# Decoder layer with windowed attention, WKV and a bit-linear MLP: the second tile's 8-bit rounding on VectorE, all calls placed anew

## The chip, the cores and the metric

The kernel runs on one core of a Trainium2 chip. The metric is the device time of one execution in microseconds; it is given as the median of several runs. TensorE (PE) multiplies, VectorE (DVE), ScalarE (ACT) and GpSimd (POOL) do the elementwise work, and SyncE (SP) only issues transfers.

## The reference

Sixteen batches of 256 tokens, 512 wide, in fp32, go through three residual steps: attention in overlapping windows of 128 tokens with sigmoid weights (16 heads of 32, one key and value head, quantised to 8 bits per batch), a WKV scan against a second input, and an MLP with ternary weights and rows quantised to 8 bits.

```python
x = x + attn(layernorm(x), wq, wk, wv, wo, ...)
x = x + wkv(w, u, layernorm(x), ctx)          # scan over 256 tokens
x = x + ffn(layernorm(x), w_gate, w_up, w_down, ln_weight)

def activation_quant(x):                       # per row, qn, qp = -128, 127
    s = qp / clip(max(abs(x), axis=-1), 1e-5)
    return clip(round(x * s), qn, qp) / s

def ffn(x):
    h = silu(bit_linear(x, w_gate)) * bit_linear(x, w_up)   # 256 x 2048
    h = ln_weight * h * rsqrt(mean(h * h) + 1e-6)
    return bit_linear(h, w_down)               # bit_linear quantises x and w
```

## The kernel before

Every engine has one program, a plain list of calls: a prologue, then `for i in range(4, B)` with 12 turns, then an epilogue. A turn works on five batches at once: b = i (queries, scores), w = i−1 (window blends, attention's output, WKV keys and scan), f = i−2 (WKV's quotient, first half of the MLP), g = i−3 (second half of the MLP), h = i−4 (output, store). The lists are written out by hand; each engine works in the order of its list, and semaphores (`Event`; `.at(f, t)` is the count that tile t of batch f brings) tie the lists together. So a call that waits holds up all that stands behind it in its list.

A batch has two tiles of 128 tokens (t = 0, 1), and the MLP's 2048 columns are four slices of 512 (n = 0 to 3). For each tile and slice: `gate_up` (TensorE, L653) makes the gate half and the up half in two banks; `silu` (ScalarE, L1022) and `hidden` (VectorE, L1526) make silu(gate)·up in `junk`; `squares` (ScalarE, L1027) sums its squares; `weigh_hidden` (GpSimd, L1858) multiplies by the norm's weight into `hid_w`. Per tile: `peak` (VectorE, L1535) takes the largest value of a row, `hidden_rstd` (GpSimd, L1875 to L1883) and `hidden_scale` (VectorE, L1542 to L1548) make the row's scale. Then `scale_hidden` (ScalarE, L996) multiplies the 128x2048 tile by it and adds MAGIC = 1.5·2^23, which rounds in fp32; `round_hidden` (ScalarE, L1006) subtracts MAGIC and writes bf16 into `hid_q`; `turn_hidden` (SP, L346) transposes a half of the tile by DMA, and `down` (TensorE, L673) multiplies. `round_hidden` of a batch must wait until the transposes of the batch before have read `hid_q`, `weigh_hidden` until the round has read `hid_w`. In the profile `hid_w`, `hid_q` and the transposed tiles all show as `work`.

Other names of the chain: `blend_windows` (L1426 to L1429) joins the attention windows, `wkv_back` (L632) transposes WKV's result, `attention_out` L613, `queries` L563, `scores` L582 (with `probs`, L957, on ScalarE); `wkv_keys` L623, `key_steps` (GpSimd, L1848), `exps` L1013, `values` L1448, `scan` L1459, `join` L1467; `rope` L1412 and `rotate` L1418 with transfers between them (`turn_queries`, L330); `keys_grid` L1398 to L1404, which needs the loads `next_keys` (L317, L318); `next_queries` (L305) loads xT once the buffer is read by `rotate(b,1)`; `weigh_windows` (GpSimd, L1841), `outputs` (GpSimd, L1889); `log_tables` (L961) loads ScalarE's table of logs. `spin(f,k,n)` (L665) makes n multiplies whose result nobody reads.

Of the kernel before, what the change touches and what calls it, by code (L numbers as in the profile page):

```python
# [14 lines left out]
NT = S // P  # L15
# [26 lines left out]
def build(nc, a, out, k_scratch, v_scratch):  # L42
# [150 lines left out]
    def event(name, per=1, unit=1):  # L193
# [62 lines left out]
    sq_sum, ms_set, h_norm, h_peak, h_scale, h_scaled, h_quant = [  # L256
        event(n, k * NT) for n, k in (("sq_sum", 1), ("ms_set", 3), ("h_norm", 1), ("h_peak", 1), ("h_scale", 4),
                                      ("h_scaled", 1), ("h_quant", 1))]
# [7 lines left out]
    def sync_program(sy):  # L266
# [72 lines left out]
        def turn_hidden(f, t, k):  # L339
            sy.wait_ge(h_quant.sem, h_quant.at(f, t))  # L340
# [41 lines left out]
        load_x(0)  # L382
        load_small()
        load_x(1)
        load_columns(0)
        load_columns(2)
        load_columns(1)
        load_x(2)
        load_x(3)
# [4 lines left out]
        store_trig(1)  # L394
        load_columns(5)
        load_x(7)
# [3 lines left out]
        load_keys(0)  # L400
        load_wq()
        load_columns(7)
        load_weights(GATE, 1)
        load_weights(GATE, 0)
        load_queries(0)
        store_trig(5)
        load_weights(GATE, 2)
        next_residual(1)
        store_trig(2)
        load_weights(GATE, 3)  # L410
        turn_queries(0, 0)
        turn_queries(0, 1)
        load_weights(UP, 0)
        load_weights(UP, 1)
        next_keys(0)
        load_weights(UP, 2)
        load_weights(UP, 3)
        next_queries(0)
        next_residual(0)
        store_trig(3)  # L420
        load_weights(DOWN, 1)
        load_weights(DOWN, 0)
        turn_queries(1, 0)
        store_trig(4)
        load_weights(DOWN, 2)
        turn_queries(1, 1)
        store_trig(6)
        load_weights(DOWN, 3)
        store_trig(7)
        next_queries(1)  # L430
        next_keys(1)
# [3 lines left out]
        turn_queries(2, 1)  # L435
        next_queries(2)
        next_keys(2)
        next_values(1)
# [3 lines left out]
        turn_queries(3, 1)  # L442
        turn_hidden(0, 0, 1)
        for i in range(4, B):
            b, w, f, g, h = i, i - 1, i - 2, i - 3, i - 4
            next_keys(w)
            next_queries(w)
            turn_hidden(h, 1, 0)
            turn_hidden(h, 1, 1)
# [4 lines left out]
            turn_hidden(g, 0, 1)  # L454
            turn_hidden(g, 0, 0)
            turn_tokens(f)
            turn_queries(b, 0)
            turn_queries(b, 1)
        turn_hidden(12, 1, 0)
        turn_hidden(12, 1, 1)  # L460
        next_values(14)
        store(12, 1)
        store(12, 0)
# [3 lines left out]
        turn_hidden(13, 1, 0)  # L467
        turn_hidden(13, 0, 0)
        turn_hidden(13, 0, 1)
        turn_tokens(15)  # L470
        turn_hidden(14, 0, 1)
        store(13, 1)
        turn_hidden(14, 0, 0)
        turn_hidden(14, 1, 0)
        turn_hidden(14, 1, 1)
        turn_hidden(15, 0, 0)
        store(13, 0)
        store(14, 0)
        turn_hidden(15, 0, 1)
        turn_hidden(15, 1, 0)  # L480
        turn_hidden(15, 1, 1)
        store(14, 1)
# [4 lines left out]
    def tensor_program(te):  # L487
# [194 lines left out]
        keys_project(1)  # L682
        keys_grow(0)
        keys_spread(2)
        keys_project(2)
# [3 lines left out]
        keys_project(4)  # L689
        keys_spread(4)  # L690
        keys_project(5)
        keys_grow(2)
        keys_spread(5)
        keys_grow(3)
        keys_project(6)
        keys_grow(4)
        query_weights()
        keys_spread(6)
        keys_grow(5)
        keys_spread(7)  # L700
        keys_project(7)
# [4 lines left out]
        spin(0, 0, 5)  # L706
        weight_total(GATE)
        scores(0, 0)
        spin(0, 0, 6)
        scores(0, 1)  # L710
        spin(0, 0, 4)
        scores(0, 2)
        scores(0, 3)
        spin(0, 0, 2)
# [3 lines left out]
        spin(0, 0, 5)  # L718
        dens(0, 2)
        nums(0, 1)  # L720
# [3 lines left out]
        spin(0, 0, 3)  # L724
        attention_out(0, 0)
        weight_total(UP)
# [1357 lines left out]
```

## Time and profile before

| | |
|---|---|
| median of 3 runs | 987.75 us (984.48 to 991.34) |
| profiled execution | 982.83 us, its span 981.5 us |
| mean granted clock | 0.991 |
| TensorE busy | 880.1 us (90%), weight loads 546.3 |
| VectorE busy | 817.0 us (83%) |
| ScalarE busy | 712.5 us (73%) |
| GpSimd busy | 428.2 us (44%) |
| chain of waits, by engine | TensorE 38%, VectorE 20%, ScalarE 17%, issue 10%, DMA 5%, GpSimd 5% |

Busy shares are means over the whole span. The chain of waits follows the work that ended last back from its end; "issue" is time in which an engine waited for nothing that the profile shows. Names in brackets behind a row of a timeline are the idle time before it and what ended that.

### The profile page before, as it was taken

How to read it: one execution, taken by the hardware profiler on the slowest of the kernel's cores; microseconds unless marked ns; L12 is line 12 of the kernel's file. 1: busy time of each engine (PE TensorE's matmuls, PEld its weight loads, DVE VectorE, ACT ScalarE, POOL GpSimd, SP SyncE). 2: the span in 40 equal slices, each digit the busy share in tenths (PEclk: the TensorE clock that was granted, in tenths of full speed). 3: DMA queues.
4: the chain of work that ended last, by engine and by line, in shares of the span. 5: the costliest groups of instructions: out<-in, count | busy, mean ns of one | idle time of the engine just before them, and what ended most of it. 6: DMA issues, size and time to landing. Idle time of an engine off the chain costs nothing.

```text
span 981.5 us, 22541 instructions
## 1 busy us (share of the span) xinstructions
PE 880.1 (90%) x8575; PEld 546.3 (56%) x8674; DVE 817.0 (83%) x1520; ACT 712.5 (73%) x1188; POOL 428.2 (44%) x507
## 2 busy tenths in 40 slices
PE   6998878888898989898989899999999998987897
PEld 3456565655565656564556555556565555653453
DVE  4677688997889898998989898989797989897953
ACT  1147384667779797978788788888888878796665
POOL 2110203454454546353636463736364544545532
PEclk9999999999999999999999999999999999999999
DMA  9996360102313333323251616243333333222033
GB/s 359 393 403 224 127 224 13 61 23 62 107 45 94 87 95 86 90 87 89 78 104 65 116 65 115 68 99 82 84 63 101 74 92 79 88 75 73 14 65 97
DMA packets 119388, 107.21 MB, mean 109 GB/s; under 512 B 91792, under 2 KB 94720, under 8 KB 118128
## 3 DMA queue, kind: packets, MB, share of 16 engines
q1 hardware_dynamic: 116320, 100.64, 35.6%
q10 hardware_dynamic: 2336, 2.52, 0.8%
q0 software_dynamic: 624, 2.59, 0.7%
q8 instruction: 69, 1.13, 0.5%
q14 instruction: 39, 0.32, 0.1%
HBM read 65.62 MB, written 10.75 MB: 78 GB/s over the span
## 4 chain that ended last, share of the span: by engine, by line
PE 38%; DVE 20%; ACT 17%; issue 10%; DMA 5%; POOL 5%; SPq 2%; DVEq 0%; ACTq 0%; POOLq 0%
PE bank L653 10%; PE bank L673 8%; PE bank L590 7%; PE bank L582 4%; ACT arena L957 3%; DVE fs L1535 2%; ACT junk L1022 2%; PE bank L563 2%; ACT work L996 2%; PE bank L613 2%; DVE rows L1436 2%; DVE amax L1504 2%; DVE stats_wkv L1492 2%; ACT junk L1027 1%; DVE junk L1526 1%
## 5 line engine op out<-in xcount | busy, mean ns | idle before, releaser
L1858 POOL TENSOR_TENSOR work<-junk,lnw 128x512 f32<-128x512 f32 x128 | 175.2, 1387 | 182.7 <-DVE junk L1526 182.2
L653 PE MATMUL bank<-w_up_gate,qT 128*128 128x512 bf16 x967 | 227.0, 381 | 18.2 <-DMA qT<-q_tok 6.8
L653 PEld LDWEIGHTS bank<-w_up_gate,qT 128*128 128x128 bf16 x1024 | 95.2, 98 | 126.5 <-DMA qT<-q_tok 9.0
L957 ACT ACTIVATE arena<-bank 128x384 f32<-128x384 f32 x256 | 104.8, 497 | 32.6 <-PE bank L582 32.5
L673 PE MATMUL bank<-w_down,work 128*128 128x512 bf16 x470 | 112.1, 381 | 17.2 <-ACT junk L1022 6.7
L1027 ACT ACTIVATE junk<-junk,deq 128x512 f32<-128x512 f32 x128 | 92.6, 723 | 41.7 <-DVE junk L1526 41.3
L1526 DVE TENSOR_TENSOR junk<-bank,junk 128x512 f32<-128x512 f32 x128 | 85.0, 680 | 41.7 <-issue 25.0
L563 PE MATMUL bank<-wide,wq_sb 128*128 128x256 f32 x512 | 116.1, 385 | 1.3 <-DVE rows L1436 1.3
L613 PE MATMUL bank<-wo_sb,wide 128*128 128x512 f32 x256 | 113.9, 597 | 1.5 <-DVE wide L1429 1.5
L996 ACT ACTIVATE work<-work,fs 128x2048 f32<-128x2048 f32 x32 | 64.0, 2001 | 67.6 <-DVE fs L1548 67.6
L563 PEld LDWEIGHTS bank<-wide,wq_sb 128*128 128x128 f32 x512 | 97.2, 192 | 24.9 <-issue 11.8
L1841 POOL TENSOR_TENSOR sums<-sums,blend 128x448 f32<-128x448 f32 x64 | 83.2, 1310 | 41.2 <-ACT sums L973 41.2
L1022 ACT ACTIVATE junk<-bank,deq 128x512 f32<-128x512 f32 x128 | 83.5, 680 | 8.7 <-PE bank L653 6.8
L582 PE MATMUL bank<-wide,k_win 32*128 32x128 f32 x1536 | 60.8, 287 | 28.5 <-ACT arena L957 18.3
L673 PEld LDWEIGHTS bank<-w_down,work 128*128 128x128 bf16 x512 | 45.8, 98 | 66.8 <-issue 7.2
L1459 DVE TENSOR_TENSOR_SCAN sums<-wkv_s,sums 128x256 f32<-128x256 f32 x128 | 79.2, 688 | 3.5 <-ACT sums L1013 3.4
L613 PEld LDWEIGHTS bank<-wo_sb,wide 128*128 128x128 f32 x256 | 48.8, 192 | 57.4 <-issue 53.7
L582 PEld LDWEIGHTS bank<-wide,k_win 32*128 32x128 f32 x1536 | 49.0, 186 | 55.4 <-ACT arena L957 37.5
L1535 DVE TENSOR_REDUCE fs<-work 128x1 f32<-128x2048 f32 x32 | 72.8, 2276 | 0.7 <-POOL work L1858 0.7
L665 PE MATMUL bank<-blend,ident 128*128 128x256 f32 x280 | 68.4, 388 | 3.6 <-ACT junk L1022 3.6
L1467 DVE SCALAR_TENSOR_TENSOR sums<-sums,wkv_s 128x512 f32<-128x512 f32 x64 | 66.3, 1094 | 0.0
L1006 ACT ACTIVATE work<-work 128x2048 bf16<-128x2048 f32 x32 | 60.7, 1901 | 0.4
(156 smaller groups left out, 1550.2 us busy)
## 6 DMA issues: line engine op xcount, KB each, us to landing
sums<-in_xT SPq DMA_DIRECT2D x8, 1024.0 KB, 9.8
wide<-in_xT SPq DMA_DIRECT2D x16, 512.0 KB, 4.6
wide<-wide SPq DMA_DIRECT2D x64, 128.0 KB, 2.1
out<-rows SPq DMA_DIRECT2D x32, 256.0 KB, 2.1
rows<-in_x SPq DMA_DIRECT2D x15, 512.0 KB, 3.6
ctx_T<-in_ctxT SPq DMA_DIRECT2D x15, 512.0 KB, 4.5
kv_b<-k_raw SPq DMA_DIRECT2D x64, 96.0 KB, 2.2
work<-in_wgT SPq DMA_DIRECT2D x4, 1024.0 KB, 13.9
```

The costliest lines, as they stand in the source:

```text
L563: last = te.matmul(in_bank(k, 2)[:, n % 2, :], wq_sb[:, c, n * P:(n + 1) * P], xT[:, c, :], start=c == 0, stop=c == NC - 1)
L582: last = te.matmul(bank[j][:, n * P:(n + 1) * P], k_win[head, window], q_cos[head, c, window], start=True, stop=True, skip_group_check=True)
L613: last = te.matmul(bank[t][:, :], heads_T[:, c, t * P:(t + 1) * P], wo_sb[:, c, :], start=c == 0, stop=c == NC - 1)
L653: last = te.matmul(bank[4 + k % 4][:, :], qT[:, c, t * P:(t + 1) * P], w_up_gate[:, m, c, cols], start=c == 0, stop=c == NC - 1)
L673: last = te.matmul(bank[6 + t][:, :], hid_T[:, t, c, :], w_down[:, c, :], start=c == 0, stop=c == NI - 1)
L957: se.activation(prob[:, :, QUAD * c + j, :], bank[j][:, 0:NW * P].rearrange("p (k q) -> p k q", k=NW), ACT.Sigmoid, scale=float(1.0 / np.s ...
L996: se.activation(hid_w[:, t, :], hid_w[:, t, :], ACT.Copy, scale=col[t]["qscale"], bias=MAGIC).then_inc(h_scaled.sem, 1)
L1022: se.activation(gated[:, n % 2, :], bank[4 + 2 * (n % 2)][:, :], ACT.Silu, scale=deq[:, 0, t:t + 1]).then_inc(silu_set.sem, 1)
L1027: se.activation(gated[:, n % 2, :], hid[:, n % 2, :], ACT.Square, scale=deq[:, 1, t:t + 1], accum_out=fs[:, t, n:n + 1]).then_inc(sq_set.s ...
L1526: ve.tensor_tensor(hid[:, n % 2, :], bank[4 + k % 4][:, :], gated[:, n % 2, :], op=ALU.mult).then_inc(hid_set.sem, 1)
L1535: ve.tensor_reduce(col[t]["am"], hid_w[:, t, :], AX.X, ALU.max, apply_absolute_value=True).then_inc(h_peak.sem, 1)
L1858: ge.tensor_tensor(hid_w[:, t, cols], hid[:, n % 2, :], lnw[:, cols], op=ALU.mult).then_inc(z_set.sem, 1)
```

## The change

Three things change. (1) The semaphore `h_quant`, one for both tiles, becomes one per tile. (2) For tile 1, `scale_hidden` on ScalarE no longer adds MAGIC, and the rounding is a new VectorE call, `hidden_round`, which adds and subtracts MAGIC in one operation and writes bf16; tile 0 stays as it was. (3) All lists of calls are reordered, in prologue, loop and epilogue. The multiplies of `spin` go from 79 to 38 ahead of the loop and from 37 to 44 behind it (two per turn in both).

```diff
-    sq_sum, ms_set, h_norm, h_peak, h_scale, h_scaled, h_quant = [
+    sq_sum, ms_set, h_norm, h_peak, h_scale, h_scaled = [
...
+    h_quant = [event(f"h_quant{t}") for t in range(NT)]
...
         def turn_hidden(f, t, k):
-            sy.wait_ge(h_quant.sem, h_quant.at(f, t))
+            sy.wait_ge(h_quant[t].sem, h_quant[t].at(f))
...
         def scale_hidden(f, t):
...
-            se.activation(hid_w[:, t, :], hid_w[:, t, :], ACT.Copy, scale=col[t]["qscale"], bias=MAGIC).then_inc(
-                h_scaled.sem, 1)
+            if t == 0:
+                se.activation(hid_w[:, t, :], hid_w[:, t, :], ACT.Copy, scale=col[t]["qscale"], bias=MAGIC).then_inc(
+                    h_scaled.sem, 1)
+            else:
+                se.activation(hid_w[:, t, :], hid_w[:, t, :], ACT.Copy, scale=col[t]["qscale"]).then_inc(h_scaled.sem, 1)
...
+        def hidden_round(f, t):
+            ve.wait_ge(h_scaled.sem, h_scaled.at(f, t))
+            if f:
+                for k in both:
+                    ve.wait_ge(hid_turned[t][k].sem, hid_turned[t][k].at(f - 1))
+            else:
+                ve.wait_ge(w_tern[DOWN].sem, w_tern[DOWN].at(0, 2))
+            ve.tensor_scalar(hid_q[:, t, :], hid_w[:, t, :], MAGIC, MAGIC, ALU.add, ALU.subtract).then_inc(
+                h_quant[t].sem, 1)
...
         def weigh_hidden(f, t, n):
...
             if f:
-                ge.wait_ge(h_quant.sem, h_quant.at(f - 1, t))
+                ge.wait_ge(h_quant[t].sem, h_quant[t].at(f - 1))
```

The order of a turn, as calls. On TensorE `gate_up(f,1,0)` moves to right behind `scores(b,3)` (it stood behind the first of the windows' sums), and `down(g,1,1)` stands between them. In the prologue, `outputs(0,1)` goes ahead of `weigh_windows(1,2)`, `hidden_rstd(0,0)` behind `weigh_windows(2,3)`, and `log_tables(1,0)`, `log_tables(2,0)` ahead of the batches' windows. Line numbers of the changed kernel differ by a few; its `hidden_round` is L1551.

VectorE, from the norm of attention's result (`wide<-rows,mv_att,rstd_att`) to the join, before:

```order
L1392 TENSOR_SCALAR wide<-rows,mv_att,rstd_att 128x512 x2
L1526 TENSOR_TENSOR junk<-bank5,junk 128x512
L1526 TENSOR_TENSOR junk<-bank7,junk 128x512
L1412 TENSOR_TENSOR wide<-bank0,kv_b 128x512 x2
L1412 TENSOR_TENSOR wide<-bank1,kv_b 128x512 x2
L1448 TENSOR_TENSOR sums<-ctx_T,sums 128x4x256
L1418 TENSOR_TENSOR wide<-wide 128x512 x2
L1459 SCALAR_TENSOR_TENSOR sums<-wkv_s,sums 128x256 x8
L1526 TENSOR_TENSOR junk<-bank5,junk 128x512
L1526 TENSOR_TENSOR junk<-bank7,junk 128x512
L1467 SCALAR_TENSOR_TENSOR sums<-sums,wkv_s 128x512 x4
```

and after:

```order
L1386 TENSOR_SCALAR wide<-rows,mv_att,rstd_att 128x512 x2
L1520 TENSOR_TENSOR junk<-bank5,junk 128x512
L1551 TENSOR_SCALAR work<-work 128x2048
L1406 TENSOR_TENSOR wide<-bank0,kv_b 128x512 x2
L1520 TENSOR_TENSOR junk<-bank7,junk 128x512
L1406 TENSOR_TENSOR wide<-bank1,kv_b 128x512 x2
L1412 TENSOR_TENSOR wide<-wide 128x512
L1442 TENSOR_TENSOR sums<-ctx_T,sums 128x4x256
L1520 TENSOR_TENSOR junk<-bank5,junk 128x512
L1412 TENSOR_TENSOR wide<-wide 128x512
L1520 TENSOR_TENSOR junk<-bank7,junk 128x512
L1453 SCALAR_TENSOR_TENSOR sums<-wkv_s,sums 128x256 x8
```

The round stands between the two first `hidden` (bank5, bank7), each `rope` is followed by other work, the last two `hidden` come ahead of the scans and `keys_grid` (L1392, L1396, L1398) ahead of the join.

ScalarE, from `scale_hidden(g,0)` to the first silu of batch f, before:

```order
L996 ACTIVATE work<-work,fs 128x2048
L1027 ACTIVATE junk,fs<-junk,deq 128x512
L1006 ACTIVATE work<-work 128x2048
L990 ACTIVATE wide<-wide,amax 128x512 x2
L996 ACTIVATE work<-work,fs 128x2048
L1006 ACTIVATE work<-work 128x2048
L1022 ACTIVATE junk<-bank4,deq 128x512
L1022 ACTIVATE junk<-bank6,deq 128x512
```

and after:

```order
L986 ACTIVATE wide<-wide,amax 128x512 x2
L993 ACTIVATE work<-work,fs 128x2048
L1005 ACTIVATE work<-work 128x2048
L996 ACTIVATE work<-work,fs 128x2048
L1021 ACTIVATE junk<-bank4,deq 128x512
L1021 ACTIVATE junk<-bank6,deq 128x512
```

The tokens' scaling (`wide<-wide,amax`) is now ahead of tile 0, and behind tile 1's scaling (L996) no rounding follows.

SP, from the tokens' transposes (`qT<-q_tok`) to the next batch's key loads, before:

```order
L337 DMA_TRANSPOSE qT<-q_tok 128x4x128 x2
L330 DMA wide<-wide 64x512 x4
L317 DMA kv_b<-k_raw 32x768 x4
L318 DMA kv_b<-v_raw 128x96
L305 DMA wide<-in_xT 128x1024
L346 DMA_TRANSPOSE work<-work 128x8x128 x2
```

and after:

```order
L338 DMA_TRANSPOSE qT<-q_tok 128x4x128 x2
L347 DMA_TRANSPOSE work<-work 128x8x128
L331 DMA wide<-wide 64x512 x4
L347 DMA_TRANSPOSE work<-work 128x8x128 x2
L306 DMA wide<-in_xT 128x1024
L347 DMA_TRANSPOSE work<-work 128x8x128
L318 DMA kv_b<-k_raw 32x768 x4
L319 DMA kv_b<-v_raw 128x96
```

Before, the key loads (`kv_b<-`) came ahead of xT's load (`wide<-in_xT`) and of the last transposes of `work`; now the first transposes stand around the queries' transfers (`wide<-wide`), and the last one and the key loads stand behind xT's load.

## Rows read from the trace of the kernel before

**Rows 1.** Chain of waits: start us, us, engine, what was written, line

```profile
287.00 2.01 ACT work L996
...
850.33 2.01 ACT work L996
```

**Rows 2.** Windows, core 0: window, length; busy PE, PEld, DVE, ACT, POOL; PEclk, DMA share, GB/s

```profile
624.00:675.00 51.00, 47.56 (x511) 29.52 (x517) 45.42 (x85) 41.94 (x71) 25.81 (x30) 1.00 0.36 87
```

**Rows 3.** Timeline of VectorE: start, us, engine, line, operation, out<-in, count [idle, releaser]

```profile
630.30 0.54 DVE L1427 TENSOR_TENSOR sums<-bank,sums 128x384 f32<-128x384 f32 x1
...
650.84 1.29 DVE L1526 TENSOR_TENSOR junk<-bank,junk 128x512 f32<-128x512 f32 x2 [2.44 <-issue]
...
657.39 0.69 DVE L1418 TENSOR_TENSOR wide<-wide 128x512 f32<-128x512 f32 x1 [0.55 <-DMA wide<-wide]
658.00 4.76 DVE L1459 TENSOR_TENSOR_SCAN sums<-wkv_s,sums 128x256 f32<-128x256 f32 x8
...
663.85 4.40 DVE L1467 SCALAR_TENSOR_TENSOR sums<-sums,wkv_s 128x512 f32<-128x512 f32 x4
```

**Rows 4.** Timeline of TensorE, the same stretch

```profile
631.01 1.04 PE L632 MATMUL bank<-ident,sums 128*128 128x128 f32 x8
...
647.84 3.40 PE L653 MATMUL bank<-w_up_gate,qT 128*128 128x512 bf16 x15
...
661.20 0.95 PE L582 MATMUL bank<-wide,k_win 32*128 32x128 f32 x24 [1.05 <-ACT arena L957]
```

**Rows 5.** Timeline of ScalarE, the same stretch

```profile
646.24 2.00 ACT L996 ACTIVATE work<-work,fs 128x2048 f32<-128x2048 f32 x1 [3.69 <-DVE fs L1548]
...
650.09 1.25 ACT L1022 ACTIVATE junk<-bank,deq 128x512 f32<-128x512 f32 x2
651.35 1.28 ACT L961 ACT_TABLE_LOAD   x1
652.65 0.72 ACT L1027 ACTIVATE junk<-junk,deq 128x512 f32<-128x512 f32 x1
```

**Rows 6.** Instructions of line L1006: ns min/median/max, first and last start, form

```profile
L1006 ACT ACTIVATE work<-work x32: 1892/1897/1911, 224.7 to 970.2; 128x2048 bf16<-128x2048 f32 x32
```

**Rows 7.** Instructions of line L1332 on w_down, the same columns

```profile
L1332 DVE TENSOR_SCALAR w_down<-work x4: 1226/1700/2176, 168.5 to 199.3; 128x2048 bf16<-128x2048 f32 x4
```

**Rows 8.** Timeline of GpSimd and VectorE, in the prologue

```profile
172.37 3.71 POOL L1848 TENSOR_TENSOR wide<-wide,grow_tab 128x512 f32<-128x512 f32 x2 [0.66 <-DVE wide L1392]
...
174.99 2.17 DVE L1332 TENSOR_SCALAR w_down<-work 128x2048 bf16<-128x2048 f32 x1
```

**Rows 9.** Timeline of GpSimd, the loop stretch of rows 3 to 5

```profile
648.03 2.73 POOL L1848 TENSOR_TENSOR wide<-wide,grow_tab 128x512 f32<-128x512 f32 x2 [0.66 <-DVE wide L1392]
```

**Rows 10.** Timeline of GpSimd and VectorE around 866

```profile
865.24 2.89 POOL L1858 TENSOR_TENSOR work<-junk,lnw 128x512 f32<-128x512 f32 x2 [6.88 <-DVE junk L1526]
...
865.67 4.17 DVE L1459 TENSOR_TENSOR_SCAN sums<-wkv_s,sums 128x256 f32<-128x256 f32 x4
...
869.76 2.71 DVE L1467 SCALAR_TENSOR_TENSOR sums<-sums,wkv_s 128x512 f32<-128x512 f32 x4
```

**Rows 11.** Timeline of SP's own queue, the loop stretch

```profile
656.05 1.84 SPq L317 DMA_DIRECT2D kv_b<-k_raw  x4
...
658.93 4.01 SPq L346 DMA_TRANSPOSE work<-work  x2
```

**Rows 12.** Transposes of line L346 in 658 to 663: issue to landing

```profile
DMA to landing us min/median/max: 5.1/5.4/5.7
```

**Rows 13.** Timeline of GpSimd in the prologue, around 208

```profile
207.40 0.30 POOL L1875 TENSOR_TENSOR fs<-fs,per_row 128x1 f32<-128x1 f32 x1
...
209.48 2.33 POOL L1841 TENSOR_TENSOR sums<-sums,blend 128x448 f32<-128x448 f32 x2
```

**Rows 14.** Timeline of TensorE around 900

```profile
900.01 3.50 PE L653 MATMUL bank<-w_up_gate,qT 128*128 128x512 bf16 x8 [4.18 <-DMA qT<-q_tok]
```

**Rows 15.** Timeline of ScalarE in the epilogue

```profile
970.20 1.91 ACT L1006 ACTIVATE work<-work 128x2048 bf16<-128x2048 f32 x1
```

More of the change, by code:

```diff
@@ L442, in sync_program @@
         turn_queries(3, 1)
+        turn_hidden(0, 1, 1)
+        turn_hidden(0, 1, 0)
+        next_queries(3)
         turn_hidden(0, 0, 1)
@@ L834, in tensor_program @@
             scores(b, 3)
-        gate_up(13, 1, 0)
-        dens(15, 0)
-        dens(15, 1)
-        dens(15, 2)
-        down(12, 1, 1)
-        nums(15, 0)
-        dens(15, 3)
+            gate_up(f, 1, 0)
+            dens(b, 0)
+            down(g, 1, 1)
+            dens(b, 1)
+            dens(b, 2)
+            nums(b, 0)
+            dens(b, 3)
         nums(15, 1)
@@ L1129, in scalar_program @@
         silu(1, 0, 0)
+        scale_hidden(0, 1)
+        silu(1, 0, 1)
         squares(1, 0, 0)
-        silu(1, 0, 1)
-        scale_hidden(0, 1)
-        exps(2)
         silu(1, 0, 2)
         squares(1, 0, 1)
+        exps(2)
         silu(1, 0, 3)
-        round_hidden(0, 1)
         probs(3, 0)
+        squares(1, 0, 2)
         probs(3, 1)
-        squares(1, 0, 2)
         probs(3, 2)
@@ L1207, in scalar_program @@
         squares(13, 1, 3)
+        scale_tokens(14)
         scale_hidden(13, 0)
-        scale_tokens(14)
         scale_hidden(13, 1)
         round_hidden(13, 0)
-        round_hidden(13, 1)
         silu(14, 0, 0)
+        silu(14, 0, 1)
         log_tables(15, 1)
         exps(15)
-        silu(14, 0, 1)
         squares(14, 0, 0)
@@ L1234, in scalar_program @@
         squares(14, 1, 2)
-        scale_hidden(14, 0)
         squares(14, 1, 3)
         scale_tokens(15)
+        scale_hidden(14, 0)
         round_hidden(14, 0)
+        silu(15, 0, 0)
         scale_hidden(14, 1)
-        silu(15, 0, 0)
-        round_hidden(14, 1)
         silu(15, 0, 1)
@@ L1597, in vector_program @@
         blend_windows(0, 1)
-        keys_grid(1)
         blend_windows(0, 2)
@@ L1667, in vector_program @@
         residual(2)
+        att_norm(2)
+        hidden(0, 1, 3)
         wkv_round(1)
-        hidden(0, 1, 3)
-        att_norm(2)
         peak(0, 1)
+        hidden_scale(0, 1)
         hidden(1, 0, 0)
-        hidden_scale(0, 1)
         hidden(1, 0, 1)
         rope(3, 0)
+        rope(3, 1)
+        hidden_round(0, 1)
+        rotate(3, 0)
+        rotate(3, 1)
+        hidden(1, 0, 2)
+        values(2)
+        hidden(1, 0, 3)
+        scan(2, 0)
         for i in range(4, B):
             b, w, f, g, h = i, i - 1, i - 2, i - 3, i - 4
-            rope(w, 1)
-            values(f)
-            rotate(w, 0)
-            rotate(w, 1)
-            scan(f, 0)
             scan(f, 1)
-            hidden(g, 0, 2)
-            hidden(g, 0, 3)
+            keys_grid(b)
             join(f)
+            peak(g, 0)
             output(h, 0)
-            keys_grid(b)
-            peak(g, 0)
+            refine(f, 0)
             output(h, 1)
-            refine(f, 0)
             quotient(f, 0)
@@ L1713, in vector_program @@
             hidden(f, 0, 0)
+            hidden_round(g, 1)
+            rope(b, 0)
             hidden(f, 0, 1)
-            rope(b, 0)
-        rope(15, 1)
-        values(14)
-        rotate(15, 0)
-        rotate(15, 1)
-        scan(14, 0)
-        hidden(13, 0, 2)
-        hidden(13, 0, 3)
+            rope(b, 1)
+            rotate(b, 0)
+            values(w)
+            hidden(f, 0, 2)
+            rotate(b, 1)
+            hidden(f, 0, 3)
+            scan(w, 0)
+        output(12, 0)
         scan(14, 1)
@@ L1780, in vector_program @@
         hidden(15, 0, 3)
+        hidden(15, 1, 0)
         peak(15, 0)
@@ L1784, in vector_program @@
         output(14, 1)
-        hidden(15, 1, 0)
         hidden(15, 1, 1)
@@ L1997, in pool_program @@
         wkv_rstd(15)
+        hidden_rstd(14, 0)
         weigh_hidden(14, 1, 3)
```

396 lines of the change are left out of this document (194 added, 202 removed).

## The prediction

> **What bounds the kernel now.** The page's shares of busy time (TensorE 90%, VectorE 83%, ScalarE 73%, GpSimd 44%) are means over stages with different limits, so I looked first for the loop's period. The chain of waits passes through the same `scale_hidden` once per batch, at 287.00 and, eleven batches later, at 850.33: (850.33 − 287.00) / 11 = 51.2 us per batch [rows 1]; the 12 turns of the loop are some 615 of the 981.5 us. One such stretch, 624 to 675, holds 47.56 us of TensorE, 45.42 of VectorE, 41.94 of ScalarE and 25.81 of GpSimd, at granted clock 1.00, the 2.4 GHz level [rows 2]. No engine is full: the turn is a ring of hand-overs, and the timelines of the engines show it. The state's transposes (L632, 631.01) start when VectorE has blended the last window (630.30 + 0.54) [rows 3, 4]. From there TensorE works through attention_out and queries with no idle time noted until gate_up(f,0,0) at 647.84 [rows 4]. VectorE stands idle for 2.44 us in front of `hidden(f,0,0)` at 650.84 and from there works back to the next blends, its largest gap 0.55 [rows 3]. So the ring is TensorE from the blend to gate_up, then VectorE from the first `hidden` to the blend. ScalarE is on it in one place: `scale_hidden(g,1)` at 646.24 for 2.00, then `round_hidden(g,1)`, then silu(f,0,0) at 650.09 [rows 5], whose result the first `hidden` needs.
>
> **What leaves ScalarE.** Sixteen roundings of 1.89 to 1.91 us [rows 6] are 30 us of its busy time. Of each only what stands ahead of the first `hidden` counts. With the round gone ScalarE is free at 648.25, but gate_up(f,0,0) starts at 647.84 and takes 3.40 for 15 multiplies, 0.22 each [rows 4]: the gate half (four) is there at 648.7, so silu ends near 649.4, and the up half (eight) at 649.6. `hidden(f,0,0)` therefore comes at 649.6 for 650.84: −1.24 us per turn, not −1.9.
>
> **What VectorE gets.** A tensor_scalar of the same size and types, 128x2048 from fp32 to bf16, is in the prologue: L1332, 1.23 us at least, 1.70 in the median, 2.18 at most [rows 7]. The one at 174.99 took 2.17, while GpSimd was in key_steps from 172.37 for 3.71 [rows 8]. In the new order the round stands behind `hidden(f,0,0)` (the order listing of VectorE), its data are ready at 648.25, so it would start near 650.25, with key_steps in the way from 648.03 to 650.76 [rows 9]. It costs 1.23 with no collision and 1.75 with the 0.5 us that is left of key_steps. The Trainium skill ("SBUF — State Buffer", section "SBUF: two separate sides") makes this a lock, held for a whole instruction by GpSimd or by VectorE in a two-port mode; by that rule the round would wait out key_steps and the turn's sum be the upper end below; the row at 174.99 agrees, and no row of before has exactly this pair.
>
> The rotates wait for a transfer behind their rope (0.55 at 657.39 [rows 3]); hidden(f,0,1), values and hidden(f,0,2) are now placed between them, so I count +0.1. `hidden(f,0,2)` and (0,3) now stand ahead of the last scans, so that GpSimd's weighing of them (L1858) falls on the scans and no longer on the join. One stretch of before shows what that does: at 865.67 four scans took 4.17 beside L1858 x2, and the join behind them 2.71 [rows 10]; usually eight take 4.76 (2.38 for four) and the join 4.40 [rows 3]. That is +1.79 − 1.69 = +0.1; I take +0.2, since two more weighings may meet the other scans.
>
> A turn then: −1.24 + 1.23 + 0.1 + 0.2 = **+0.3** with no collision at the round, +0.8 with it, +0.9 with a little more at the rotates. Nearest to the new place is the row with the collision, but it is in the prologue; I take **+0.6** between them: 12 × 0.6 = **+7.2 us**.
>
> **The other moves in a turn.** scale_tokens goes ahead of scale_hidden(g,0): 1.3 us earlier for the tokens' transposes, as much later for tile 0, whose down has its multiplies only after the scores; nothing. gate_up(f,1,0) moves up between the scores and the windows' sums and can fill gaps of TensorE such as the 1.05 at 661.20 [rows 4]; VectorE's chain sets the end there, so I count 0 (it is the term of the faster rival). On SP's queue `turn_hidden(g,1,0)` now stands behind `next_queries`, which must wait for rotate(b,1), and the key loads behind both. Before, the key loads issue at 656.05 and the transposes of tile 0 and 1 at 658.93, behind the xT load [rows 11], and these land after 5.1 to 5.7 us [rows 12]. I count 0 and make it the slower rival.
>
> **Edges.** Prologue: outputs(0,1) passes one window weighing, 2.33 / 2 = 1.2 us for one [rows 13], on a stretch where GpSimd is on the chain: −1.2. hidden_rstd(0,0), four operations from 207.40 to 209.48, no longer stands in front of the last two window weighings, which are on the chain: −2.1 [rows 13]. Two table loads leave batch 1's windows; one takes 1.28 (651.35), and the next activation starts at 652.65, 0.02 after it [rows 5]. There ScalarE has room to wait, so I count 0 of a possible −2.6. The Trainium skill ("ScalarE: Activation LUTs", section "What ACT_TABLE_LOAD costs") adds a drain, which makes a switch some 2.66 us; by it the two would be worth 5.3. The row at 652.65 shows no drain, and the row decides. Of the 79 spins ahead of the loop 41 go; they do no work but hold the clock up. If it falls once more, a row prices it: after 4.18 us idle eight multiplies took 3.50 us [rows 14], where eight take 1.8 at 0.22 each, so 1.7; at a chance of one in four, +0.4. Epilogue: the last round, at 970.20 for 1.91 [rows 15], has nothing beside it and becomes 1.23: −0.7. The one of batch 14, as long, leaves the front of a silu of batch 15; of its 1.9 I take −1.3, as TensorE gates the silu there too. Sum: −1.2 − 2.1 + 0.4 − 0.7 − 1.3 = **−4.9**; with everything in full (tables 2.6) −8, with nothing of it, 0.
>
> **The sum.** +7.2 − 4.9 = +2.3 on the profiled execution's 982.83: 985.1. The median of the three runs is 987.75 (984.48 to 991.34), 4.9 above that execution; put on it, 990. The edges' bound reaches 3 further down than their value, so I say **989**. About 1% is what a measurement of this kernel can tell from no change (the three runs spread by 0.7%), and this is inside it.
>
> **Rival A, faster (0.26): VectorE has the room.** A turn holds 45.42 us of VectorE; 46.7 with the round, of 51 [rows 2]. If the round falls into the time that VectorE now idles ahead of `hidden` (2.44 [rows 3]) or is made good by a later wait that goes, and no collision shows, the ring is TensorE's with ScalarE: of TensorE's 51.0 − 47.56 = 3.4 us of gaps [rows 2] the earlier gate_up(f,1,0) takes about the one of 1.05 in front of the scores [rows 4], 0.95 as I count it. 12 × −0.95 = −11.4, with the edges −16.3: 971. For it: ScalarE does lose 1.9 us exactly in front of silu. Against it: VectorE's largest gap from 650.84 to the blends is 0.55, so what is put in there is paid there.
>
> **Rival B, slower (0.24): SP's queue makes the keys late.** Behind next_queries (near 659) and one transpose, 2.0 of issue, the key loads go out near 661 in place of 656.05 [rows 11]; beside the xT load, where the transposes take 5.1 to 5.7 [rows 12], they land at 666.4 to 667. keys_grid stands in front of the join now: scans 658.00 + 4.76 [rows 3], plus the two `hidden` at 0.65 each, the scans' 1.8 of contention and the 0.6 make 666.4. VectorE then waits up to 0.7 on its own chain, and the transpose of g's second tile, as late, holds TensorE's down(g,1,0) back by some 0.5. With the +0.6: 1.8 × 12 − 4.9 = +16.7: 1004. It decides from one point: whether the keys land before VectorE is through its scans. Against it: the keys are small transfers, and may not share the 5 us of the transposes.
>
> That the change does not do what it says is excluded: in the order listings each batch has one 128x2048 round on VectorE and one fewer on ScalarE.
>
> **How the numbers follow.** Forecast 0.50, its own range 983 to 999 (turns +3.6 to +10.8, edges −8 to 0). A 0.26, spread 965 to 979; B 0.24, spread 998 to 1010. To leave out no more than 0.2 the range reaches into both: 968 to 1004. Against the 1% bounds, 977.9 and 997.6: faster 0.27, same 0.48, slower 0.25.
>
> **What the profile after would show.** A period in the chain of 51.5 to 52.1 (A: near 50.3; B: 52.7 or more). The idle time ahead of `hidden(f,0,0)` down from 2.44 to about 1.2. The round at 1.23, or longer or late beside L1848. No wait for the DMA in front of keys_grid (B: 0.5 or more). L1006 on ScalarE sixteen times, 30 us. The step most likely to fail is that VectorE closes the ring all the way: if a wait for TensorE or a transfer further on goes away by the new placing, the +0.6 is absorbed and A holds.

## The result

The changed kernel takes 995.7 us in the median of 18 runs (988.2 to 1000.62); the kernel before takes 986.2 in the median of 18 (17 of them 982.38 to 991.34, one 2163.38). The ratio is 1.009, with a 95% interval of 1.0075 to 1.0105: slower by 0.9%. That is inside the range and inside the 1% that was called "same", but clear of the measurement's noise. The profiled execution took 996.26 us, its span 994.9 against 981.5. The two profiled executions are 13.4 us apart and the medians 9.5, mostly because the profiled one of the kernel before is 3.4 us faster than its median.

Two rows of ScalarE's timeline give the period, as [rows 1] did; both are `scale_hidden(g,1)`, eleven batches apart:

```profile
292.57 2.00 ACT L996 ACTIVATE work<-work,fs 128x2048 f32<-128x2048 f32 x1 [1.21 <-DVE fs L1542]
...
865.78 2.01 ACT L996 ACTIVATE work<-work,fs 128x2048 f32<-128x2048 f32 x1 [1.21 <-DVE fs L1542]
```

(865.78 − 292.57) / 11 = 52.11 us per turn, for 51.21. So of the 13.4 us between the two profiled spans the eleven turns have 0.90 × 11 = 9.9. The first of these rows, called the start of the loop below, comes 5.6 later (292.57 for 287.00), and from the last of them to the end it is 2.05 shorter (129.12 for 131.17).

A window of one turn (columns as in [rows 2]):

```profile
636.00:687.00 51.00, 48.46 (x518) 29.54 (x510) 46.26 (x86) 40.46 (x69) 27.48 (x30) 1.00 0.33 88
```

VectorE has 0.84 us more than in [rows 2], ScalarE 1.48 less, TensorE 0.9 more. Where the turn waits is in VectorE's timeline of the same stretch, which answers to [rows 3]:

```profile
661.64 0.69 DVE L1520 TENSOR_TENSOR junk<-bank,junk 128x512 f32<-128x512 f32 x1 [1.02 <-PE bank L655]
662.25 1.81 DVE L1551 TENSOR_SCALAR work<-work 128x2048 bf16<-128x2048 f32 x1
664.24 1.29 DVE L1406 TENSOR_TENSOR wide<-bank,kv_b 128x512 f32<-128x512 f32 x2 [0.18 <-PE bank L625]
...
668.21 0.69 DVE L1412 TENSOR_TENSOR wide<-wide 128x512 f32<-128x512 f32 x1 [0.89 <-DMA wide<-wide]
...
678.53 0.65 DVE L1392 TENSOR_SCALAR kv_b<-kv_b,grid 128x256 f32<-128x256 f32 x2 [0.46 <-DMA kv_b<-v_raw]
...
679.85 2.73 DVE L1461 SCALAR_TENSOR_TENSOR sums<-sums,wkv_s 128x512 f32<-128x512 f32 x4
```

The first row is `hidden(f,0,0)`: the idle time ahead of it fell from 2.44 to 1.02, and it now waits for TensorE. The round (L1551) takes 1.81 with key_steps beside it. `keys_grid` at 678.53 waits for the keys' DMA, which [rows 3] never did. Here it is 0.46; over eleven turns it is 0.33 to 2.30, 1.39 in the mean. Behind the wait everything keeps its distance: the next blend of the last window comes 11.70 to 11.73 us after the start of the join's last operation, in each of the eleven turns. The chain of waits, which shows what was last (start, us, what), goes straight through it:

```profile
670.60 0.69 DVE wide L1412
671.29 0.02 issue
671.31 0.48 SPq L306
...
671.88 1.24 SPq L347
...
675.21 3.29 DMA kv_b<-v_raw
678.50 0.03 issue
678.53 0.66 DVE kv_b L1392 x2
```

rotate(b,1) (L1412) lets xT's load out (L306), behind that the last transpose (L347), behind that the keys. TensorE has a wait of the same kind, for the transposed tile in front of `down` (L675), in 9 of the 11 turns, 0.30 to 1.47 (before in 2, 0.31 and 0.43):

```profile
625.54 1.89 PE L675 MATMUL bank<-w_down,work 128*128 128x512 bf16 x8 [0.43 <-DMA work<-work]
```

In the changed kernel this wait is off the chain: the 11.70 to 11.73 are the same in the turns with it and in the two without.

The keys also take longer to land once they are issued. This is line L318 of the changed kernel within 300 to 890 us; the row that matters is the last, from issue to landing:

```profile
L318 SPq DMA_DIRECT2D kv_b<-k_raw x44: 408/422/461, 307.4 to 830.0; - x44
...
DMA to landing us min/median/max: 3.2/4.1/5.1
```

and the same transfer in the kernel before:

```profile
L317 SPq DMA_DIRECT2D kv_b<-k_raw x40: 413/422/450, 348.0 to 810.6; - x40
...
DMA to landing us min/median/max: 2.1/2.2/2.4
```

Median 4.1 us for 2.2: they run beside the xT load, which was issued 1.9 to 4.4 us ahead of them; before, it was issued behind them.

### The profile page after: what moved, and what is told of

It is laid out like the page before. It is cut to its first block, busy times and chain, and to the rows that moved or that the text cites. A ratio compares the mean times of both kernels' runs of the same rounds, so it can differ in the third digit from the quotient of the medians.

```text
span 994.9 us, 22505 instructions
## 1 busy us (share of the span) xinstructions
PE 888.7 (89%) x8606; PEld 543.8 (55%) x8606; DVE 833.9 (84%) x1536; ACT 689.8 (69%) x1173; POOL 450.5 (45%) x507
## 4 chain that ended last, share of the span: by engine, by line
PE 40%; ACT 18%; DVE 14%; issue 11%; DMA 9%; SPq 5%; POOL 4%; DVEq 0%; ACTq 0%; POOLq 0%
PE bank L565 10%; PE bank L615 10%; PE bank L655 7%; DMA kv_b<-v_raw 3%; ACT sums L964 3%; ACT junk L1021 3%; PE bank L675 2%; DVE sums L1461 2%; PE bank L497 2%; DMA work<-work 2%; PE bank L584 2%; ACT junk L1026 2%; SPq L347 2%; POOL sums L1898 2%; ACT sums L969 2%
## 5 line engine op out<-in xcount | busy, mean ns | idle before, releaser
L655 PE MATMUL bank<-w_up_gate,qT 128*128 128x512 bf16 x1024 | 240.5, 381 | 8.4 <-DVE rows L1556 2.8
L1867 POOL TENSOR_TENSOR work<-junk,lnw 128x512 f32<-128x512 f32 x128 | 192.0, 1515 | 113.3 <-DVE junk L1520 113.3
L675 PE MATMUL bank<-w_down,work 128*128 128x512 bf16 x512 | 121.2, 382 | 13.3 <-DMA work<-work 11.1
L584 PE MATMUL bank<-wide,k_win 32*128 32x128 f32 x1536 | 66.3, 306 | 44.0 <-ACT arena L953 25.0
L1453 DVE TENSOR_TENSOR_SCAN sums<-wkv_s,sums 128x256 f32<-128x256 f32 x128 | 98.0, 832 | 0.8 <-ACT sums L1012 0.7
L584 PEld LDWEIGHTS bank<-wide,k_win 32*128 32x128 f32 x1536 | 53.7, 202 | 70.7 <-ACT arena L953 40.9
L1884 POOL TENSOR_TENSOR fs<-fs,per_row 128x1 f32<-128x1 f32 x32 | 6.2, 193 | 185.8 <-DVE fs L1527 185.8
L675 PEld LDWEIGHTS bank<-w_down,work 128*128 128x128 bf16 x512 | 45.9, 98 | 69.7 <-issue 13.7
L1898 POOL TENSOR_TENSOR sums<-sums 128x512 f32<-128x512 f32 x32 | 40.8, 1276 | 45.6 <-ACT sums L979 45.6
L986 ACT ACTIVATE wide<-wide,amax 128x512 f32<-128x512 f32 x32 | 21.3, 714 | 56.7 <-DVE amax L1502 56.7
L592 PE MATMUL bank<-arena,one_win 128*32 128x128 f32 x1536 | 56.1, 283 | 2.3 <-ACT arena L953 2.3
```

The costliest lines, as they stand in the source:

```text
L584: last = te.matmul(bank[j][:, n * P:(n + 1) * P], k_win[head, window], q_cos[head, c, window], start=True, stop=True, skip_group_check=True)
L655: last = te.matmul(bank[4 + k % 4][:, :], qT[:, c, t * P:(t + 1) * P], w_up_gate[:, m, c, cols], start=c == 0, stop=c == NC - 1)
L675: last = te.matmul(bank[6 + t][:, :], hid_T[:, t, c, :], w_down[:, c, :], start=c == 0, stop=c == NI - 1)
L1453: ve.tensor_tensor_scan(state[:, c, n, 1:S + 1], sc["decay"][:, c:c + 1].to_broadcast([P, S]), GG[:, c, n, :], 0.0, ALU.mult, ALU.add).the ...
L1867: ge.tensor_tensor(hid_w[:, t, cols], hid[:, n % 2, :], lnw[:, cols], op=ALU.mult).then_inc(z_set.sem, 1)
```

## The experiments

Period, wait and start of the loop are from the profiled execution of each: the period and the start by the rows of `scale_hidden(g,1)` as above, the wait ahead of `keys_grid` as the mean of the eleven turns. A single profiled execution can differ from the median, in its start above all (see the prologue).

| kernel | median us | against before [95%] | period | wait for keys | loop starts |
|---|---|---|---|---|---|
| before | 986.2 | 1 | 51.21 | 0 | 287.0 |
| changed | 995.7 | 1.009 [1.0075, 1.0105] | 52.11 | 1.39 | 292.6 |
| e5, before, round alone on VectorE | 991.0 | 1.0058 [1.0037, 1.0079] | 51.62 | 0 | 288.9 |
| e3, changed, round on ScalarE | 1002.3 | 1.0168 [1.0149, 1.0186] | 52.06 | 1.38 | 295.6 |
| e1, keys alone earlier | 1023.7 | 1.0407 [1.0365, 1.045] | 55.2 | 0 | 287.9 |
| e9, last transpose alone earlier | 993.7 | 1.0058 [1.0037, 1.008] | 51.92 | 1.20 | 291.0 |
| e6, both earlier | 979.5 | 0.9926 [0.9901, 0.995] | 50.83 | 0.09 | 287.4 |
| e7, e6 with round on ScalarE | 989.4 | 1.0014 [0.9996, 1.0033] | 51.05 | 0.03 | 289.5 |
| e11, e6 with the round later | 981.6 | 0.9933 [0.991, 0.9955] | 50.91 | 0.02 | 292.5 |
| e11b, changed, keys_grid behind the join | 987.4 | 1.0003 [0.9985, 1.0021] | 51.39 | 0 | 287.8 |
| e12b, e6 and e11b together | 977.5 | 0.9918 [0.9897, 0.9939] | 50.78 | 0 | 289.0 |
| e4, changed, spins back | 996.6 | 1.0112 [1.0091, 1.0134] | 52.08 | 1.36 | 290.2 |
| e10, e6 with spins | 980.2 | 0.992 [0.9894, 0.9945] | 50.80 | 0 | 292.2 |
| e8, changed, first loads as before | 995.0 | 1.0084 [1.0059, 1.0109] | 52.20 | 1.50 | 293.8 |

**The round, one part at a time.** e5 makes only this part of the change in the kernel before, in the loop as shown and alike in prologue and epilogue:

```diff
             hidden(f, 0, 0)
+            hidden_round(g, 1)
             hidden(f, 0, 1)
             rope(b, 0)
...
             scale_hidden(g, 1)
-            round_hidden(g, 1)
```

> The kernel before, all calls as they were, with the rounding of tile 1 alone moved to VectorE, behind hidden(f,0,0), and a semaphore per tile. Round theory (the prediction's sum for this part): -1.24 for the earlier hidden, +1.23 to +1.8 for the round, so +0 to +0.6 a turn: 986 to 994, against 986 of the kernel before. Its rival: VectorE absorbs the round where it idles, the turn falls by 0.6 or more, 979 or less.

+0.41 us a turn, +0.6% in time: the total is what the prediction's sum allowed, but little of it stands where the sum has it. Behind the last blend, rope(b,0) comes after 22.11 us for 22.01 before (means of eleven turns), so the earlier `hidden` and the round together come to +0.10. Another 0.12 is there by the end of the join, mostly from two turns in which rotate(b,1) came late, and 0.20 lies behind the join: in 5 of the 11 turns an operation of VectorE beside GpSimd's weighing of the windows took 1.65 to 1.67 us for 0.68 (before in one), such as

```profile
318.08 1.67 DVE L1472 TENSOR_TENSOR sums<-sums 128x512 f32<-128x512 f32 x1
```

e3 does the opposite, in the changed kernel (`scale_hidden` adds MAGIC for both tiles again, and prologue and epilogue are treated alike):

```diff
             scale_hidden(g, 1)
+            round_hidden(g, 1)
...
             hidden(f, 0, 0)
-            hidden_round(g, 1)
```

> The changed kernel with the rounding of tile 1 put back on ScalarE, behind its scaling, all other calls where the change has them. Round theory: VectorE loses the round (1.81 us), the first hidden comes 1.24 later again, so the turn falls by 0.6 and the time by 7 us to about 989. Keys theory: the keys' loads hang on rotate(b,1), which comes 0.6 earlier with everything ahead of it; keys_grid still waits 1 to 1.5 us in the mean, the period is 51.5 to 52, the time 988 to 995; what stays above the kernel before is the wait.

It is slower than the changed kernel by 6.6 us, and both theories missed the time (989; 988 to 995). Yet its period is the same, 52.06 for 52.11, nearly what the keys theory had (51.5 to 52). From the last blend to the first `hidden` it is 1.45 longer in the mean, from there to the next blend 1.5 shorter, and keys_grid waits 1.38 as before. So in the new order the round's place doesn't set the period; the keys do. The 6.6 us are the edges: the loop starts 3.0 later, the epilogue is 3.6 longer (132.8 us from the last row to the end for 129.1). There the round on ScalarE is in front of other work.

**SP's queue.** e1 moves one call of the loop (and its like in front of it):

```diff
-            next_keys(w)
...
             turn_hidden(g, 1, 1)
+            next_keys(b)
             next_queries(b)
             turn_hidden(g, 1, 0)
```

> The changed kernel with one call of SP's list moved: the next batch's key loads go out ahead of xT's load and the last transpose of tile 1, and no longer behind them. Keys theory: in the changed kernel VectorE waits 0.33 to 2.30 us for the keys in front of keys_grid in every turn, 1.4 in the mean; without that wait the turn is 52.1 - 1.4 = 50.7 us, so the wait disappears, the period of the chain is 50.6 to 51.0 and the time about 980 (-13 to -17 us against the changed kernel), below the kernel before. Round theory (the prediction's own sum): the loss is the round on VectorE, which stays; then the end of the wait only shows another one behind it, the period stays at 51.8 or more and the time at 991 or more.

Both theories missed: 28 us slower than the changed kernel. The wait of VectorE did go; the row has no idle time:

```profile
695.17 0.62 DVE L1393 TENSOR_SCALAR kv_b<-kv_b,grid 128x256 f32<-128x256 f32 x2
```

but the keys' five issues (2.3 us) now stand in front of xT's load and the last transpose, and TensorE waits for that transpose in every turn, 2.2 to 4.1 us:

```profile
696.64 2.80 PE L676 MATMUL bank<-w_down,work 128*128 128x512 bf16 x7 [2.68 <-DMA work<-work]
```

`down(g,1,0)` stands ahead of scores(b,3) in TensorE's list, so all of the batch's windows are late. The two transfers behind rotate(b,1) both matter, and xT's load, which is needed 30 us later, does not. e6 acts on that:

```diff
-            next_keys(w)
...
             turn_hidden(g, 1, 1)
-            next_queries(b)
             turn_hidden(g, 1, 0)
+            next_keys(b)
+            next_queries(b)
```

> The changed kernel with SP's list mended at both calls: behind turn_hidden(g,1,1) come turn_hidden(g,1,0), the key loads, and xT's load last. In the run where the keys alone moved, keys_grid waited no more, but the last transpose went out 2.4 us later, behind keys and xT, and TensorE waited for it 2.2 to 4.1 us in every turn. Keys theory: here both go out ahead of xT, keys some 0.9 us earlier than in the changed kernel and with nothing of xT in front; keys_grid waits 0.3 or less, TensorE does not wait for the transpose, the period is 50.7 to 51.1, the time 980 to 984, below the kernel before. Rival (bandwidth): three transposes in a row keep the queues busy, the keys land as late as in the changed kernel, the period stays at 51.6 or more and the time at 990 or more.

979.5 us: 16 less than the changed kernel, and less than the kernel before. The period is 50.83, the wait 0.09, and TensorE waits for no transpose in the loop. The keys land after 2.4 us again:

```profile
L318 SPq DMA_DIRECT2D kv_b<-k_raw x44: 412/421/443, 301.7 to 811.5; - x44
...
DMA to landing us min/median/max: 2.1/2.4/3.4
```

e9 moves only the transpose ahead of xT and leaves the keys behind it:

> The changed kernel with the last transpose of tile 1 ahead of xT's load; the key loads stay behind xT's, as in the changed kernel. Late-issue theory: the keys wait because they go out late behind rotate(b,1), whatever is in front; they go out at the same time or 1 us later than before, keys_grid still waits 1 us or more, and only TensorE's wait for the transpose (11 us in all) goes: 988 to 994. Crowding theory: xT's load in front of transpose and keys is what delays, the wait falls only when the keys pass xT too; here it is as large as in the changed kernel, the same time range, but the keys land more than 3 us after they are issued, as there.

TensorE's waits in the loop are gone, the wait for the keys stays at 1.20, and they land as slowly as the crowding theory wants (the answer for L318):

```profile
DMA to landing us min/median/max: 3.2/3.7/4.0
```

The time is 993.7, 2 less than the changed kernel, and the period falls by 0.19, as much as the wait for the keys does; TensorE's waits were worth nothing there. So the loss in the loop is the keys. In e6 the last of the key loads lands 35.07 us behind the last blend, in the changed kernel 37.06 (means); VectorE is there at 35.7. Of these 1.99 us, 0.70 is that it goes out earlier and 1.29 that it lands faster with no xT load in front. No run separates the two; added up, the earlier issue alone would leave 0.7 us of the wait and the faster landing alone 0.1 (an estimate from these means). e11b leaves SP alone and moves the one who waits:

```diff
-            keys_grid(b)
             join(f)
+            keys_grid(b)
             peak(g, 0)
```

> The changed kernel, SP's list as it is, with keys_grid put back behind the join in the loop (one call moved on VectorE). Keys theory: the wait for the keys is a matter of both ends; the join (2.7 us) fills it, the keys are not needed before set_keys 17 us later, so the wait falls from 1.4 to about 0, the join comes 1.3 to 2.7 us earlier, and the period is 50.7 or less: 978 or less. If only the late SP queue costs (the transposes, the xT load) and not the wait of VectorE, the time stays at 993 or more.

The wait of VectorE is 0 and the time falls by 8 us, to that of the kernel before; the period is 51.39, not 50.7, since TensorE still waits for the transpose (0.36 to 1.38 in 10 turns). Now this wait is on the chain: from the last start of the join to the next last blend it takes 13.15 us in the turn without it and 13.30 to 14.41 in the others. The two expectations each had half of it. Both mends together:

> Both mends: SP's order transposes, keys, xT, and keys_grid behind the join. keys_grid takes 1.3 us (0.65 + 0.34 + 0.34) that stand ahead of the join on VectorE's chain in the mended kernel; behind it they run while ScalarE and GpSimd work. If the join closes the ring there, the period falls from 50.8 to 49.5 to 50.0 and the time from 979.5 to 964 to 971; if VectorE's own length sets the end (it must do keys_grid anyway before the blends), nothing moves, 978 to 981.

Nothing more: 50.78 for 50.83, 977.5 for 979.5 with overlapping intervals. `join` came 1.4 us earlier and no one used it.

**What sets the end once the waits are gone.** e7:

> The same mended order of SP, with tile 1's rounding on ScalarE. Keys theory: in the changed order the round on ScalarE makes blend to hidden 1.4 us longer and hidden to blend 1.4 shorter, so that, the wait gone, the period is again 50.7 to 51.1; only prologue and epilogue lose (6 us as measured without the mended order): 986 to 990. Round theory: the period falls by a further 0.4 or more, as VectorE is spared 1.8 us, and the time is 983 or less.

989.4. The period is 51.05, 0.2 more than with the round on VectorE, so the round theory (0.4 less) is out; the rest of the 9.9 us between the two is again prologue and epilogue. e11 moves the round to where VectorE idles:

```diff
             hidden(f, 0, 0)
-            hidden_round(g, 1)
             rope(b, 0)
             hidden(f, 0, 1)
             rope(b, 1)
+            hidden_round(g, 1)
             rotate(b, 0)
```

> The kernel with SP's order mended, and in the loop the round on VectorE moved from behind hidden(f,0,0) to behind rope(b,1), ahead of rotate(b,0), where VectorE waits 0.9 us for the rope's transfer in every turn. If VectorE's chain closes the ring, the turn falls by 0.5 to 0.9 (50.8 to 50.0 to 50.3) and the time to 969 to 974. If the round there collides with GpSimd for its whole length or makes the transposes of tile 1 and the keys late, the period stays at 50.8 or rises, 979 or more.

No gain: 50.91. The timeline of VectorE shows why:

```profile
654.73 1.29 DVE L1407 TENSOR_TENSOR wide<-bank,kv_b 128x512 f32<-128x512 f32 x2 [1.91 <-PE bank L626]
...
657.73 1.32 DVE L1552 TENSOR_SCALAR work<-work 128x2048 bf16<-128x2048 f32 x1
```

The round takes 1.32 there and not 1.81, but rope(b,0) (the row at 654.73) cannot start before TensorE's transposes of the WKV keys (L626): it idles 1.91, and starts 2.60 us after `hidden(f,0,0)`, exactly as in e6 with the round in that gap. Measured from the last blend, rope(b,0) starts 21.85 us later in the kernel before (630.30 [rows 3] to 652.15), in the changed one (642.38 to 664.24) and in e6; in the mean of eleven turns 22.01, 21.86 and 21.85. The round on VectorE was put into a hole. The hole could be seen in the trace of the kernel before, where the same transposes (L623) end at 652.12, 0.03 us ahead of rope(b,0):

```profile
651.08 1.04 PE L623 MATMUL bank<-ident,wide 128*128 128x128 f32 x8
...
652.15 2.48 DVE L1412 TENSOR_TENSOR wide<-bank,kv_b 128x512 f32<-128x512 f32 x4
```

A first `hidden` that comes 1.24 us earlier could not move rope(b,0) by more than that. Later in the turn the chain of e6 is TensorE's, without a gap from 658.08 to the product of the next half with its silu (`hidden`, 676.39; scores L585, down L676, gate_up L656):

```profile
653.99 1.04 PE bank L585 x24
...
658.08 0.95 PE bank L585 x24
...
659.03 1.83 PE bank L676 x8
...
664.46 1.83 PE bank L656 x8
...
674.53 1.85 PE bank L656 x8
...
676.39 0.68 DVE junk L1521
```

**The prologue.** The granted clock of the changed kernel is low in two stretches, where before it was 1.00 and 0.93:

```profile
75.00:100.00 25.00, 14.98 (x215) 12.12 (x217) 16.13 (x21) 16.12 (x27) 0.00 (x0) 0.73 0.78 268
125.00:150.00 25.00, 13.60 (x161) 11.15 (x163) 21.48 (x32) 19.01 (x35) 1.11 (x1) 0.70 0.52 176
```

e4 puts 35 idle multiplies back around the scores of batches 0 and 1.

> The changed kernel with 35 idle multiplies put back around the scores of batches 0 and 1 in the prologue (8 and 15 ahead of the first score, 1, 4, 4 and 4 more between the scores). Clock theory: the 5.6 us that the changed kernel is behind at the start of the loop are in good part TensorE at half clock (granted 0.73 in 75 to 100 us, 0.70 in 125 to 150, where before shows 1.00 and 0.93); with them the granted clock there is 0.9 or more, the loop starts 2 to 4 us earlier, the time is about 993. Rival: the chain there is VectorE's and ScalarE's, TensorE's slower multiplies lie in waits; the clock comes back, the time does not move (within 1 us).

The clock comes back:

```profile
75.00:100.00 25.00, 18.34 (x275) 15.02 (x274) 16.95 (x24) 18.10 (x31) 0.00 (x0) 1.00 0.79 271
125.00:150.00 25.00, 21.65 (x241) 18.25 (x243) 20.49 (x31) 20.73 (x37) 0.00 (x0) 0.88 0.56 178
```

and the time does not move (996.6 against 995.7). The profiled execution of e4 does start its loop 2.4 us earlier than that of the changed kernel, as the clock theory had it, but its median shows none of it, and e10 shows the opposite, on top of e6:

> The kernel with SP's order mended (transposes, keys, xT) and the 35 idle multiplies put back in the prologue. Clock theory: now that the loop is no longer bound by the keys, the prologue's clock shows, 2 to 3 us: 977. Rival: the prologue's chain is not TensorE's there, within 1 us of 979.5.

980.2 for 979.5, with the loop's start 4.7 us later in the profiled execution. e8 gives back the old order of the first loads:

> The changed kernel with the first eight calls of SP's list as in the kernel before (the small tables second, xT's pairs in the old order). TensorE's first multiply was at 12.40 us in the changed kernel and 7.30 before. If these 5 us are on the path of the prologue, the loop starts 4 to 5 us earlier and the time is 991; if the transfers of the inputs, whose engines are full to 75 us, set the pace there, nothing moves (within 1 us of the changed kernel).

The first multiply is 3 us earlier (9.38), the loop is not (293.8). What does show is scatter. The prologues of the changed kernel and of e11b are the same, and their loops start at 292.6 and 287.8. The parting begins at TensorE, which is 2.94 us without work and is then granted a clock of 0.50, the 1.2 GHz level, over 221 to 226 us:

```profile
221.39 1.94 PE L634 MATMUL bank<-ident,sums 128*128 128x128 f32 x8 [2.94 <-DVE sums L1421]
223.12 2.34 PE L655 MATMUL bank<-w_up_gate,qT 128*128 128x512 bf16 x5
```

where e6, with the same calls up to there, is granted 1.00 over 219 to 224 and has

```profile
219.27 1.06 PE L635 MATMUL bank<-ident,sums 128*128 128x128 f32 x8 [0.51 <-DVE sums L1422]
220.18 1.89 PE L656 MATMUL bank<-w_up_gate,qT 128*128 128x512 bf16 x8
```

In the changed kernel's run VectorE came 2 us later to that blend, most of it through operations that took longer beside GpSimd (L1398 1.21 us for 0.34, L1474 1.56 for 0.69). Of the twelve profiled executions with the changed prologue or nearly it, seven (the changed kernel, e3, e4, e8, e9, e10, e11) have this wait of 2.80 to 2.94 us, then a granted clock of 0.50 to 0.73 in the 5 us that follow, and attention_out starts 3.9 to 5.2 us behind the transposes of L634; their loops start at 290.2 to 295.6. The other five (e1, e6, e7, e11b, e12b) have 0.51 or 0.52, 1.00 and 2.63, and start at 287.4 to 289.5. So the late start is not a cost that every execution pays, and this third fall of the clock, which no run took away by itself, costs 1.3 to 2.5 us where it comes.

## Why the prediction was right, and where it was not

The number held (995.7 in 968 to 1004; 0.9% slower, called "same"), the working less so, and that the two go together is partly luck: the range reaches into both rivals, the forecast was 989, 1.3 above the median it started from, and the kernel lost 9.5. Of the signs, the period (52.11, foreseen 51.5 to 52.1), the idle time ahead of `hidden(f,0,0)` and the round came as foreseen; the wait for the DMA in front of keys_grid, which was to be absent, is rival B's.

- *`hidden(f,0,0)` 1.24 us earlier.* From the blend it came 20.54 us later before, 19.25 after: −1.3. Right, and for the reason given: it now waits for TensorE's gate_up.
- *The round at 1.23 to 1.75.* 1.81 or 1.82 in all twelve turns of the loop, 1.22 and 1.23 where GpSimd is still:

```profile
L1551 DVE TENSOR_SCALAR work<-work x16: 1217/1810/2067, 249.1 to 984.2; 128x2048 bf16<-128x2048 f32 x16
```

  It is as a lock would have it: key_steps (660.24 + 2.73) ends at 662.97, the round, begun at 662.25, at 664.06, and GpSimd's next weighing, begun at 662.93, takes 2.26 where one takes 1.28. Over the rounds of the changed kernel, e5 and e11 that begin with 0.2 to 1.0 us of one GpSimd operation still to go, the round takes what is left of it plus 1.08 or 1.09 (0.24 left: 1.33; 0.58: 1.67; 0.73: 1.81; 0.98: 2.07). The Trainium skill ("SBUF — State Buffer", section "SBUF: two separate sides") makes the port that the two engines share an exclusive lock, held for a whole instruction by GpSimd or by VectorE in a two-port mode, and the trace agrees.
- *VectorE closes the ring from the first `hidden` to the blend.* This step failed for the new order. rope(b,0) waits for TensorE at the same 21.85 us, so the round cost nothing there (with it on ScalarE the turn is 52.06 for 52.11 in e3, and 51.05 for 50.83 in e7), and with the waits gone TensorE's own list is the chain later on. "What is put in there is paid there" fails even for the order before, where both `hidden` stand ahead of rope: e5's +0.41 lies within the +0.3 to +0.9, but only 0.10 of it is at rope(b,0). The +0.6 a turn was for the wrong thing. So was the +0.2 for scans and join: scans 6.26 for 4.76 and join 2.73 for 4.40 are −0.2.
- *SP's queue, counted at 0.* This is the step that made the loss. As rival B it had the right mechanism and place: keys behind next_queries and a transpose, landing late, `keys_grid` waiting. Sized at up to 0.7, the wait measured 1.39. The 0.5 for `down(g,1,0)` is there too (0.30 to 1.47 in 9 turns), but it doesn't add to the other: it is off the chain until the keys are mended (e11b). What the rival said against itself, that keys might not share the transposes' delay, was wrong: 4.1 us for 2.2.
- *Rival A, a turn of 50.3.* A ring that TensorE closes is what e6 and e12b show with the waits gone, 50.8: the new order is worth −0.4 a turn, not −0.95. The gap of 1.05 that gate_up(f,1,0) was to fill is not filled; it is there in every turn of e6, as in

```profile
658.08 0.95 PE L585 MATMUL bank<-wide,k_win 32*128 32x128 f32 x24 [1.05 <-ACT arena L954]
```

  Which of the moved calls brings the −0.4 was not tested. In the changed kernel the wait for the keys took it back and 0.9 more. Forecast and outcome agree because +0.6 for the round, which cost nothing, stood where +0.9 belonged, −0.4 for the order and +1.3 for the wait. That is luck.
- *Edges −4.9.* The epilogue's −2.0 measured −2.05, most of it where it was priced: from scale_hidden(14,1) to scale_hidden(15,1) 25.13 us for 26.35 (−1.2, priced −1.3), from there to the end −0.6 (priced −0.7). The prologue's −2.9 did not come: +5.6 in the profiled run, +0.4 to +2.5 in the five experiments e1, e6, e7, e11b and e12b, which miss the late stretch (287.4 to 289.5 for 287.0). Its moves were not tested one by one, so which of them failed stays open. The clock was priced at +0.4. Where it fell early it cost nothing that e4 or e10 could give back; the fall at 221 us cost 2.5 in the profiled run. On the medians, 11 × 0.90 − 2.05 = +7.9 of the +9.5 are accounted for by the eleven turns and what follows; the 1.6 left is of the size of those +0.4 to +2.5.

## What to carry to other kernels

When calls are reordered, follow every transfer to who needs it next and when: a load that nobody needs for 30 us, put in front of two that are needed in 5, cost 1.3 us a turn here, more than moving 1.8 us of work between engines gave or took (0.2 between e6 and e7, 0.4 between e5 and the kernel before). Before pricing work added to an engine, find what releases the operation behind it; if that is another engine at a fixed time, the slot is free. And a wait can be cured at either end, but each of two late transfers has to be cured: in e11b the second one, harmless until then, held the kernel at 987.4, and in e1 moving one ahead of the other made the kernel 28 us slower.

## What the runs showed of the hardware

- A key load of 96 KB (four go out in a row) lands 2.1 to 2.4 us after its issue in the kernel before and 2.1 to 3.4 in e6, where no 512 KB load goes ahead of it (at most 3.8 in e1). It takes 3.2 to 5.1 in the changed kernel (1.9 to 4.4 us behind xT's 512 KB load) and 3.2 to 4.0 in e9 (0.8 to 2.1 us behind it).
- One and the same VectorE operation (128x2048, fp32 to bf16) takes 1.22 us alone and, begun while a GpSimd tensor_tensor has 0.24, 0.73 or 0.98 us to go, 1.33, 1.81 or 2.07. The profile shows the wait as duration, not as idle time.
- Two stretches of 25 us of prologue at a mean granted clock of 0.73 and 0.70 in place of 1.00 and 0.88 cost nothing measurable (995.7 against 996.6 us). A fall to 0.50 over 221 to 226 us, where TensorE had been idle for 2.94 us, put attention_out 2.5 us further behind the transposes than in e6 at 1.00.
